# M of the ca attention in 80 woven products stored as sums, other staging places for g, and the last batch in another order

## The reference

```
query = x @ Wq;  keyt = enc @ Wk;  valt = enc @ Wv
hs    = mha(query, keyt, valt)                  # softmax(q k^T / sqrt(80)) v, head by head
ca_q1 = einsum('btc,th->bch', ca, Wq_ca)[:, indices, :]
ca_hs1 = mha(ca_q1, x, x)
ca_q2 = ca_hs1 @ Wq;  ca_k2 = ca @ Wk_ca;  ca_v2 = ca @ Wv_ca
ca_hs2 = mha(ca_q2, ca_k2, ca_v2)
out   = (hs + ca_hs2) @ Wout + b_out + x
```

## Time and profile before

| | |
|---|---|
| median of 3 runs (lowest, highest) | 975.27 us (973.79, 976.19) |
| the profiled execution, its own time | 974.73 us |
| its span in the profile | 973.0 us |
| PE busy | 960.6 us, 99% of the span |
| DVE, ACT, POOL busy | 701.8, 491.6, 343.0 us |
| moved by DMA | 195.21 MB, mean 201 GB/s |

### The profile page before, as it was taken

One profiled execution on the slowest core, in us unless ns is written; L12 is line 12 of the kernel. 1 busy time (PEld: TensorE's weight loads), 2 busy tenths in 40 slices (PEclk: granted clock), 3 DMA queues, 4 the chain that ended last, 5 costly groups with the idle time before them and its releaser, 6 DMA issues.

```text
span 973.0 us, 21012 instructions
## 1 busy us (share of the span) xinstructions
PE 960.6 (99%) x6634; PEld 943.3 (97%) x6634; DVE 701.8 (72%) x1260; ACT 491.6 (51%) x911; POOL 343.0 (35%) x302
## 2 busy tenths in 40 slices
PE   9999899999999999999999999999999999999998
PEld 8999899999999999999999999999999999998998
DVE  5545677777777777787777787777777777876445
ACT  6534556454555555564646363736464545555111
POOL 5223363334343425160615152433333343415000
PEclk9999999999999999999999999999999999999999
DMA  8989987797779777768796879788887978797455
GB/s 266 301 276 264 285 193 213 163 225 176 201 182 206 185 198 185 198 186 193 194 193 194 190 195 185 209 174 218 175 221 163 217 174 206 178 207 183 116 170 167
DMA packets 157625, 195.21 MB, mean 201 GB/s; under 512 B 81056, under 2 KB 111712, under 8 KB 157600
## 3 DMA queue, kind: packets, MB, share of 16 engines
q1 hardware_dynamic: 150000, 181.53, 75.9%
q10 hardware_dynamic: 7600, 13.35, 4.4%
HBM read 82.74 MB, written 19.95 MB: 106 GB/s over the span
## 4 chain that ended last, share of the span: by engine, by line
PE 91%; DMA 3%; SPq 2%; DVE 1%; ACT 1%; POOL 1%; issue 0%; ACTq 0%; POOLq 0%
PE psS L780 24%; PE psB L815 18%; PE psB L820 9%; PE psS L755 8%; PE psT L796 6%; PE psS L930 5%; PE psT L848 4%; PE psT L854 3%; PE psB L825 2%; PE psB L827 2%; PE psB L981 2%; DMA kstack<-kT 1%; PE psS L1055 1%; PE psB L903 1%; PE psB L880 1%; PE psT L855 1%
## 5 line engine op out<-in xcount | busy, mean ns | idle before, releaser
L780 PE MATMUL psS<-encT_keep,Wk_keep 128*128 128x360 f32 x1440 | 254.1, 329 | 0.0
L780 PEld LDWEIGHTS psS<-encT_keep,Wk_keep 128*128 128x128 f32 x1440 | 237.5, 188 | 0.7
L1190 ACT ACTIVATE probs<-psS,negmax 100x718 f32<-100x718 f32 x128 | 110.1, 860 | 131.8 <-DVE negmax L1612 131.7
L815 PE MATMUL psB<-PT_h,encN_h 128*128 128x400 f32 x480 | 169.5, 353 | 0.0
L815 PE MATMUL psB<-PT_l,encN_h 128*128 128x400 f32 x480 | 165.6, 345 | 0.0
L635 POOL TENSOR_TENSOR encT_keep<-encT_raw,encT_keep 128x718 fp32r<-128x718 f32 x45 | 83.6, 1857 | 180.7 <-ACT encT_keep L1219 176.2
L1629 DVE TENSOR_TENSOR PT_l<-psT,PT_h 128x600 fp32r<-128x600 f32 x128 | 99.6, 778 | 40.5 <-ACT PT_h L1201 36.8
L626 POOL TENSOR_TENSOR Mbd<-Mbd,fmask 128x320 fp32r<-128x320 f32 x48 | 41.8, 871 | 213.3 <-DMA Mbd<-m_split 210.7
L1612 DVE TENSOR_REDUCE negmax<-psS 100x1 f32<-100x720 f32 x128 | 114.8, 897 | 1.3 <-PE psS L755 1.3
L1201 ACT ACTIVATE PT_h<-psT 128x600 fp32r<-128x600 f32 x128 | 85.7, 669 | 42.7 <-PE psT L796 38.9
L1623 DVE TENSOR_SCALAR probs<-probs,inv 100x718 f32<-100x718 f32 x128 | 102.1, 798 | 4.5
(11 more groups left out here) (259 smaller groups left out, 1787.4 us busy)
## 6 DMA issues: line engine op xcount, KB each, us to landing
kstack<-kT SPq DMA_DIRECT2D x64, 448.8 KB
kstack<-kT SPq DMA_DIRECT2D x192, 112.2 KB
enc_raw<-in_encN_dram SPq DMA_DIRECT2D x48, 384.0 KB, 4.6
encT_raw<-in_encT_dram SPq DMA_DIRECT2D x45, 359.0 KB, 3.9
kstack<-kT SPq DMA_DIRECT2D x32, 359.0 KB
kstack<-kT SPq DMA_DIRECT2D x32, 269.2 KB
kstack<-kT SPq DMA_DIRECT2D x32, 179.5 KB, 3.5
kstack<-kT SPq DMA_DIRECT2D x64, 89.8 KB, 3.8
```

The lines of the kernel that those rows point to most:

```text
L780: mm = pe.matmul(keys_in(f, first)[:, half, 0:HALF], w[:, c, f * 128:(f + 1) * 128], e[:, c, k0:k0 + HALF], start=(j == 0), stop=(j == 3 * ...
L815: pe.matmul(psB[:, 1, 0:RH], eN[0][:, k, cc], PT[p][:, k, rows], start=(k == 0 and p == 0), stop=False)
L1190: nc.scalar.activation(halves(P[h % PRING][0:S, 0:KEYS]), without_overlap(psS[score_slot[h]], S), ACT.Exp, bias=negmax[:, h:h + 1], accum_ ...
```

## The change

It has these parts, in the order of the program:

- **v2** (`ca_values`): the high part of ca is no longer multiplied alone but together with the low part, side by side. So 12 matmuls take the place of 18, the result is the sum of two halves of the PSUM rows, and ACT and DVE make that sum before they split it. ACT splits head 1 and head 2 later, and head 2 on DVE comes after k2.
- **M in 80**: high and low of k2 lie side by side, so each piece is one matmul on 128 columns and one on 64. They are woven, four behind every three matmuls, into the queries (1,1), (1,2), (1,4) and (1,5).
- **M as sums**: two DVE reductions for each of the five pieces (`m_sum`) add the two halves; ACT's five `m_high` and DVE's five `m_low` are gone. M is stored once in float32 (half the bytes), into `kT` first, and each batch loads half as much. POOL then splits it in each batch (a copy and a subtraction more in `spread_m`).
- **Order of stage 1**: `query(2, 1)` comes ahead of `keys(0, 0)`. On SP the load of heads 3 to 5 comes ahead of the second store of q, the loads of x, ahead of the store of v2, and so on. `keys(0, 0)` is split by ACT only when four of the five stores of M have landed.
- **g's places**: g of group 2 is staged in `PT`, in its last slot and the other half of the columns, and g of group 3 in `Wv`. Their stores have semaphores of their own, and ACT's first `pt_high` waits for the stores of q alone.
- **Batch 0**: `b2_pt_high(0, 1)` and `b2_pt_low(0, 1)` come ahead of `expo(0, 4)` and `rowmax(0, 4)`.
- **Last batch**: on SP the load of Wout comes first and the last third of enc comes behind the lifts; on PE `context(15, 0)` comes behind `turn(15, 4)`, the second scores and `scores(15, 7)`; on ACT two splits of Wout come later. The input tiles of the last product are split into `kstack` instead of `kT`.

The diff, cut to what these parts need:

```diff
-    m_d = nc.dram_tensor("m_split", [FT, 128, B, 2, HT], F32R).ap()
+    m_d = nc.dram_tensor("m_sums", [FT, 128, B, HT], F32).ap()
...
+        m_raw = raw(Mbd[:, :, 1, 0:HT])
...
+        k2T_both = kst_keep[0:D, 2 * CT * H:2 * CT * H + 2 * HEADS * B * T].rearrange("d (h n) -> d h n", h=HEADS)
+        k2T = [k2T_both[:, :, p * B * T:(p + 1) * B * T] for p in range(2)]
...
+        m_sums = [raw(kT_keep[:, c * B * HT:(c + 1) * B * HT]) for c in range(FT)]
...
+            if j == FT and g == 2:
+                return PT_keep[p][rows, KT - 1, HALFCOLS]
+            if j == FT and g == 3:
+                return Wv_s[p][rows, 0, 0:GT]
...
                 def store_m(c):
-                    wait_apart(sp, s["mlo"], c + 1, s["passed_sp"])
-                    sp.dma_start(raw(m_d[c].rearrange("f b a n -> f (b a n)")), raw(mst[c])).then_inc(s[f"mst{c // 2}"], 16)
+                    wait_apart(sp, s["msum"], FT + c + 1, s["passed_sp"])
+                    sp.dma_start(m_d[c].rearrange("f b n -> f (b n)"), m_sums[c]).then_inc(s[f"mst{c // 2}"], 16)
...
                 def spread_m(b):
-                    pool.wait_ge(s["min"], 16 * b + 16)
+                    wait_apart(pool, s["min"], 16 * b + 16, s["passed_pool"])
+                    high, low = Mbd[:, :, 0, 0:HT], Mbd[:, :, 0, HT:2 * HT]
+                    nc.gpsimd.tensor_copy(high, m_raw).then_inc(s["mbd"], 1)
+                    pool.wait_ge(s["mbd"], 5 * b + 1)
+                    nc.gpsimd.tensor_tensor(low, m_raw, high, ALU.subtract).then_inc(s["mbd"], 1)
+                    pool.wait_ge(s["mbd"], 5 * b + 2)
...
-                        for k, (w, k2) in enumerate(products(wqT[h % WRING], k2T)):
-                            mm = pe.matmul(ps_m(c)[:, h * B * T:(h + 1) * B * T], w[:, c * 128:(c + 1) * 128],
-                                           k2[:, h, :], start=(k == 0), stop=(k == 2))
+                        if h >= HEADS // 2:
+                            pe.wait_ge(s["msum"], c + 1)
+                        o, cc = m_head(c, h), slice(c * 128, (c + 1) * 128)
+                        pe.matmul(o, wqT[h % WRING][0][:, cc], k2T_both[:, h, :], start=True, stop=False)
+                        mm = pe.matmul(o[:, 0], wqT[h % WRING][1][:, cc], k2T[0][:, h, :], start=False, stop=True)
...
-                for j in range(NP):
-                    query(1, j)
-                    m_parts(parts[j], parts[j + 1])
+                for j, m in enumerate((None, 0, 10, None, 20, 30)):
+                    query(1, j, m)
                 query(2, 0)
+                query(2, 1)
                 pe.wait_ge(s["wlo"], 5)
-                pe.wait_ge(s["mlo"], 2)
+                pe.wait_ge(s["msum"], FT + 2)
                 keys(0, 0, first=True)
-                query(2, 1)
...
                     if first and h == 0:
-                        act.wait_ge(s["qst2"], 16 * 8)
+                        act.wait_ge(s["qst2"], 16 * 6)
...
                         act.wait_ge(s["mst0"], 16 * 2)
+                        act.wait_ge(s["mst1"], 16 * 2)
...
+                def m_sum(a, c):
+                    dve.wait_ge(s["m"], HEADS // 2 * (a + 1))
+                    nc.vector.tensor_reduce(
+                        m_sums[c].rearrange("f (b a n) -> f b a n", b=B, a=2)[:, :, a],
+                        ps_m(c).rearrange("f (k b n) -> f b n k", k=2, b=B), AX.X, ALU.add).then_inc(s["msum"], 1)
```

212 lines of the change are left out of this document (109 added, 103 removed).

## The result

| | before | changed |
|---|---|---|
| median of 16 runs each | 974.4 us | 982.9 us |
| lowest, highest | 972.0, 981.19 | 976.6, 991.29 |
| ratio, 95% interval | | 1.0069 [1.0047, 1.0092] |
| profiled execution, span | 973.0 us | 985.9 us |
| span's mean granted clock | 0.996 | 0.984 |

The ratio and its interval leave out the run of 991.29 us, which is over 1.5% above the fastest; the quotient of the two medians is 1.0087. The change made the kernel slower, where 973.2 us (967.5 to 977) was forecast. The runs of the changed kernel don't lie around one value. They follow the granted clock: the seven quickest, at 976.6 to 979.5 us, have a mean clock of 0.991 to 0.995, and the nine others, at 982.9 to 991.3 us, 0.983 to 0.991.

What follows compares the result with a forecast made beforehand. PE was taken as the bound, busy for 960.6 of 973.0 us. Terms -0.7 - 1.9 + 0.5 + 0 = -2.1 us on 974.73 us gave 972.6; the median stands 0.54 above, so 973.2 us, range 967.5 to 977.

Steps and rivals of the forecast that it cites:

- I get PE's last M at 53 us: Stage 1: PE's last product of M at 53 us, leading to lifts of piece 0 at 64.2 against 65.3 us.
- the first term: Stage 1: PE has 6.9 us less to do before the keys of batch 0, of which about 0.7 us arrives.
- Wait 0 to 2.6 us, take 1.: Stage 1: PE waits for DVE's first reductions before the second half of M, entered as 1 us.
- PE's own work: Stage 1: 40 fewer M matmuls at 108 ns save 4.3 us, 6 fewer in ca_values save 0.9 us.
- denser mix: Stage 1: denser PE work should avoid the fall of the clock near 32 us, saving 1.7 us.
- The chain: From the first lifts at 65.34 us to the scores, SP and the DMAs take 17.2 us, without PE.
- -1.9 us for g's places: Batch 0: ACT's first pt_high no longer waits for g's store, so PE's wait of 1.96 us goes, 1.9 us gained.
- +0.5 us for the swap: Batch 0: putting P1T's split ahead of the maximum lengthens the chain ending at 110.70 us by 0.5 us (0 to 1).
- Together 0: Last batch: the wait for lifts goes, turn(15, 4) waits 2.5 to 3.2 us; net 0 (0.9 gained to 3 lost).
- the rival's mechanism: Last batch: ACT, held by the late third of enc, reads hs late and PE stalls, +4.6 us; chance 0.1.
- POOL holding DVE up: Loop: POOL's two new operations slow DVE, 0.5 us in each of 16 batches, ending at 981 us; chance 0.02.
- the signs that the prediction had named for being wrong: Lifts starting before 62.5 us, M matmuls in groups of four not at 108 ns, or PE idle inside the loop.

Runs made afterwards that it cites:

- e15: The changed kernel without an edit, run again on another chip: median 983.42 us, ratio 1.0084 to the kernel before.
- e17: e16 with the whole last batch of the changed kernel: median 974.91 us, ratio 1.0024 to the kernel before.
- e13: The kernel before, with PE waiting for the split of query (1,2) ahead of the third block of M: median 980.81 us, ratio 1.0083.
- e14: The kernel before, with a PE wait added behind query (1,3) that was over when PE came, so no gap: median 971.47 us, ratio 0.9990.
- e18: The kernel before, with PE waiting for the split of heads 5 behind query (1,2), a gap of 1.26 us: 974.7 us, ratio 1.0014.
- e16: The kernel of e8 again, on another chip: median 970.73 us, ratio 0.9974 to the kernel before.
- e7: e6 with ACT's first pt_high waiting for the stores of g of group 2 again: median 972.19 us, ratio 0.9987 to the kernel before.
- e6: The changed kernel with the last batch in its earlier order and DVE's five first reductions of M moved ahead of two splits: median 972.03 us, ratio 0.9980.
- e3: The changed kernel with M's products in four blocks of 20 behind the queries instead of woven into them: median 976.45 us, ratio 1.0036.
- e8: e6 with batch 0 in its earlier order (expo and rowmax ahead of P1T's split): median 970.46 us, ratio 0.9970 to the kernel before.
- e4: The changed kernel with four of DVE's first reductions of M ahead of the split of heads 5, the fifth behind it: median 977.0 us, ratio 1.0036.
- e2: The changed kernel with the last batch's load of the last third of enc ahead of the last lifts again: median 976.82 us, ratio 1.0050.
- e10: e8 with the changed kernel's last batch, but the load of the last third of enc early: median 972.81 us, ratio 1.0008 to the kernel before.
- e11: e8 with only SP's changed order of the last batch, the last third of enc late: median 972.95 us, ratio 0.9995 to the kernel before.

## Why the prediction was wrong, step by step

**"I get PE's last M at 53 us" failed, and with it the first term.** It was 58.1 us in the changed kernel. The step before it had named the wait: "The second half of M waits for DVE's first reductions ... Wait 0 to 2.6 us, take 1." It was 1.30 us (1.30 and 1.31 in the profiles of the four kernels that had it unchanged), so the wait was sized well. The failed step is that it was entered at its own length: behind it came up to 17 us at half clock, 8.5 us of time. Closing the gap (with batch 0 as before) was worth 8.5 us in the median, e15 to e17.

**PE's own work was forecast well, the credit for the clock was not.** The woven products run at 0.112 us each where 0.108 were entered, and v2's matmuls take 1.86 us instead of 2.69, 0.8 us less where 0.9 were entered. The wait of 0.5 us for the heads 3 to 5 didn't come: PE waits nowhere for over 0.2 us between 24 and 42 us. But the 1.7 us that the "denser mix" should save at 32 us were no property of the kernel before: e13, e14 and e18 don't have that fall, without any weaving.

**The chain was read rightly, but its head was taken for safe.** The 17.2 us from the first lifts to `scores(0, 1)` don't hold PE (the prediction took these for the first scores); the reasoning that PE's saving does not arrive was right for a saving and was not turned round for a loss. PE stands at the head of the chain, with its product of the keys (what ACT's split followed in e13) or with M's last product and the stores of M (what it waited for in the changed kernel), so there PE's delay passes in full.

**With the gap closed the forecast of this part came true.** In e16 the steps can be held against the numbers: PE's last M at 50.7 us (forecast 53), DVE's sums until 54.5 us (forecast 56), lifts of piece 0 from 64.0 us (forecast 64.2), PE waiting 4.29 us before the first scores (forecast 4 and more). The timeline of SP's queue of e16:

```profile
56.34 3.81 SPq L448 DMA_DIRECT2D m_sums<-kT  x5
64.00 0.74 SPq L393 DMA_DIRECT2D kstack<-kT  x1
```

And e16's timeline of PE:

```profile
75.31 0.38 PE L762 MATMUL psS<-kstack,qstack_h 120*100 120x360 f32 x1 [4.29 <-DVE kT L1655]
...
107.64 0.42 PE L990 MATMUL psB<-encN_h,Wv_h 128*128 128x400 f32 x1 [1.61 <-DVE PT_l L1787]
```

Its median is 2.8 us below the kernel before, where the sum without the swap and the last batch was -0.7 - 1.9 = -2.6 us. The total fits better than its terms, which is luck in part: the 1.7 us of clock in the first term and the 1.9 us of the second are not shown.

**-1.9 us for g's places: gone in the changed kernel's trace, not shown in the time.** PE's wait of 1.96 us at 101 us is gone in the changed kernel. But e7, which has the wait on the store back, is as quick as e6 (972.19 and 972.03 us). The landing of 8.1 us, on which the term rested, was 5.3 us in e7. In e13 and e18, where g is staged as before, PE waits 0.35 us at this place. And in e3, where g is staged as in the change, the wait is back: the last store of q landed only after 11.9 us. e3's timelines of ACT and of PE:

```profile
97.00 0.67 ACT L1218 ACTIVATE PT_h<-psT 128x600 fp32r<-128x600 f32 x1 [2.73 <-DMA q_split<-PT_l]
```

```profile
101.34 0.45 PE L992 MATMUL psB<-encN_h,Wv_h 128*128 128x400 f32 x1 [2.00 <-DVE PT_l L1790]
```

A wait on a landing is only as long as that landing is in one execution. PE then waited longer in the next place (1.76 us at 115.25 us against 0.97 us).

**+0.5 us for the swap: neither shown nor contradicted.** e8 to e6 is 1.6 us in the median with overlapping intervals, and the waits before `query(3, 4)` overlap (2.02 and 1.54 us with the swap, 1.20 and 1.61 us without).

**"Together 0" for the last batch: the order of events was right, the sum was not.** PE's wait came out at 3.01 us in e15 and e17 (2.5 to 3.2 forecast), but at 3.53, 3.62 and 6.42 us in e3, e4 and the changed kernel; the wait for lifts went. What was wrong is the credit: "`turn(15, 5)` comes at about 890.9 against 891.34 us". The price is 4.2 us (e16 to e17, in the median). The waits and the fall of the clock behind `turn(15, 4)`, entered only as a possibility, are the rule: all five profiles with the whole changed last batch (the changed kernel, e3, e4, e15, e17) show it, and neither of the two with the early third of enc (e2, e10). And in the profiled execution the third of enc landed 7.9 us after its issue (4.6 us in e11), which is the rival's mechanism with its own price of 6.42 us.

**POOL holding DVE up: seen in stage 1, but it didn't make the gap.** In the loop it cost nothing that the profile shows. In stage 1, SP loads x of group 2 earlier, and POOL's splits of it now run from 39.6 to 45.7 us beside DVE's split of the heads 5, which took 1.68 instead of 0.82 us, ahead of the reductions PE waited for. DVE's timeline of the changed kernel:

```profile
40.92 1.68 DVE L1794 TENSOR_TENSOR kstack<-probs,kstack 80x640 fp32r<-80x640 f32 x1
42.59 0.57 DVE L1788 SCALAR_TENSOR_TENSOR PT_l<-psB,PT_h 128x400 fp32r<-128x400 f32 x1
43.08 1.28 DVE L1799 TENSOR_REDUCE kT<-psS 128x256 f32<-128x512 f32 x2
```

The same split in the kernel before:

```profile
40.81 0.82 DVE L1778 TENSOR_TENSOR kstack<-probs,kstack 80x640 fp32r<-80x640 f32 x1
```

The extra 0.86 us looks like two thirds of the gap, but it is none of it. What stands next on DVE, the split of query (1,2), needs ACT's part of the same query, and that was ready only at 42.56 us; DVE began it at 42.59 us. ACT's timeline of the changed kernel:

```profile
42.07 0.49 ACT L1335 ACTIVATE PT_h<-psB 128x400 fp32r<-128x400 f32 x1
```

So the gap comes from the order, as the prediction had it: the reductions stand behind the split of query (1,2), and that behind ACT's splits of x. Only in e4, where the fifth sum follows the slowed split at once, does PE wait for it. The Trainium skill ("SBUF — State Buffer", the part on ports) has DVE and GpSimd take turns on a shared pair of ports; the row of 1.68 us agrees, and the reductions beside the same POOL work (1.28 us for two, 0.64 each, as forecast) were not slowed.

In sum, e16 is 2.8 us below the kernel before, the last batch adds 4.2 us and the gap 8.5 us, which makes the 9.9 us by which e15 lies above it. The direction was wrong for one reason then: both losses are gaps of PE that were seen, most of them sized nearly rightly at 1 to 3 us, and booked without what the clock does behind them. None of the signs that the prediction had named for being wrong came (lifts before 62.5 us, another pace of M; PE idle in the loop for a few tenths only); what came was the lifts almost 7 us later than forecast, for which it had named none.

## What to carry to other kernels

Where PE is at 99%, price a new gap by the gap and by the clock that may fall behind it, and as a chance, not as a fixed sum: the same gap of 1.3 us had 0, 6.8 and 17 us of half clock behind it in different executions. For the same reason a fall of the clock in one profile is no saving that a change can be credited with before a second profile shows it too. Time that PE saves ahead of a chain of stores and landings is lost in a wait, but time that it loses at the head of that chain arrives in full. Before a slowed instruction is blamed for a wait, look at what the next one on that engine was waiting for. And when a change gives several groups of run times, read each run's granted clock before looking for the cause in the median; here moving five DVE instructions (with batch 0's earlier order beside it) was worth 8.5 us, more than all the matmuls that the change saved.
